# Scores and maxima in half-row form: two heads stacked in each half of the rows, maxima in neighbouring pairs

## The reference, cut to what matters

```python
q = (query @ Wq + bq).reshape(B, Nq, H, D).transpose(0, 2, 1, 3)   # H = 16 heads, D = 8
k = (key_value @ Wk + bk).reshape(B, Nkv, H, D).transpose(0, 2, 1, 3)
attn = jnp.einsum('bhqd,bhkd->bhqk', q, k) * scale
attn = jax.nn.softmax(jnp.clip(attn, -CLAMP, CLAMP), axis=-1)
x = jnp.einsum('bhqk,bhkd->bqhd', attn, v).reshape(B, Nq, Cq) @ Wo + bo
```

## Time and profile before

| what | value |
|---|---|
| time, median of 3 runs | 981.94 us (979.5 to 982.6) |
| profiled execution, its span | 981.2 us |
| span from the median | 0.7 us less |
| busy TensorE, VectorE, ScalarE, GpSimd | 934.3, 737.5, 647.0, 350.3 us |
| cross-attention | periods of some 22 us from about 70 us to about 770 us |

### The profile page before, as it was taken

The page is one execution under the profiler, slowest core; times in us unless marked ns, Lnnn a source line. Parts: engine busy times, 40 slices in busy tenths (PEclk is TensorE's granted clock), DMA queues, the critical chain, the costliest instruction groups (busy, mean ns, idle before and its releaser), DMA issues.

```text
span 981.2 us, 28874 instructions
## 1 busy us (share of the span) xinstructions
PE 934.3 (95%) x10535; PEld 753.6 (77%) x10535; DVE 737.5 (75%) x1426; ACT 647.0 (66%) x1081; POOL 350.3 (36%) x334
## 2 busy tenths in 40 slices
PE   6877999999999999999999999999999899999995
PEld 4645787877777777787777877778777678999894
DVE  6673777777777777777777777777788857777996
ACT  3654777777777777777777777777776444445554
POOL 6452352223233332222323333222231413112992
PEclk8897999999999999999999999999999899999998
DMA  6538566666555556666655555666654201002331
GB/s 140 116 75 197 119 143 135 145 136 138 131 118 118 118 125 138 140 136 137 136 128 118 118 118 128 140 138 137 138 121 96 66 1 44 23 22 83 130 113 41
DMA packets 43626, 111.45 MB, mean 114 GB/s; under 512 B 15491, under 2 KB 26053, under 8 KB 43461
## 3 DMA queue, kind: packets, MB, share of 16 engines
q1 hardware_dynamic: 43572, 110.77, 49.9%
HBM read 32.23 MB, written 1.89 MB: 35 GB/s over the span
## 4 chain that ended last, share of the span: by engine, by line
PE 90%; DVE 4%; ACT 2%; SPq 2%; issue 1%; DMA 1%; POOL 0%; ACTq 0%; DVEq 0%
PE psum L1590 18%; PE psum L1414 18%; PE psum L1655 13%; PE psum L1421 8%; PE psum L1426 8%; PE psum L1659 4%; PE psum L1682 3%; PE psum L1683 2%; PE psum L1684 2%; PE psum L1695 2%; PE psum L1694 2%; PE psum L1696 2%; PE psum L1545 1%; PE psum L1431 1%; SPq L395 1%
## 5 line engine op out<-in xcount | busy, mean ns | idle before, releaser
L946 DVE TENSOR_REDUCE arena<-psum 128x1 f32<-128x500 f32 x672 | 443.0, 671 | 176.9 <-PE psum L1414 176.7
L759 ACT ACTIVATE arena<-psum 125x896 f32<-125x896 f32 x384 | 348.1, 916 | 114.2 <-PE psum L1590 102.5
L1414 PE MATMUL psum<-K_hi,Q_bd 128*128 128x500 f32 x672 | 310.0, 470 | 7.0 <-DVE arena L946 4.2
L547 POOL TENSOR_TENSOR arena<-arena,K_hi 128x500 fp32r<-128x500 f32 x96 | 119.9, 1249 | 407.3 <-ACT K_hi L690 407.3
L1590 PE MATMUL psum<-Q_st,K_st 97*125 97x224 f32 x1536 | 243.7, 281 | 0.7 <-ACT arena L759 0.6
L1590 PEld LDWEIGHTS psum<-Q_st,K_st 97*125 97x125 f32 x1536 | 222.7, 190 | 23.1 <-issue 3.9
L1414 PEld LDWEIGHTS psum<-K_hi,Q_bd 128*128 128x128 f32 x672 | 128.2, 191 | 64.9 <-issue 27.1
L1655 PE MATMUL psum<-arena 125*25 125x168 f32 x3072 | 171.2, 313 | 0.2
L813 ACT ACTIVATE K_st<-psum 128x448 fp32r<-128x448 f32 x128 | 69.7, 544 | 79.2 <-PE psum L1684 77.7
L1659 PE MATMUL psum<-arena 125*9 125x56 f32 x3072 | 117.7, 214 | 0.0
L1659 PEld LDWEIGHTS psum<-arena 125*9 125x9 f32 x3072 | 94.5, 92 | 16.7
(11 more groups left out here) (250 smaller groups left out, 1052.4 us busy)
## 6 DMA issues: line engine op xcount, KB each, us to landing
K_st<-K_hi SPq DMA_DIRECT2D x256, 187.5 KB, 4.7
K_st<-arena SPq DMA_DIRECT2D x128, 187.5 KB, 3.4
arena<-in_ctx SPq DMA_DIRECT2D x32, 562.5 KB, 6.7
arena<-gate_rows SPq DMA_DIRECT2D x8, 896.0 KB, 4.4
arena<-in_L_ffn_W SPq DMA_DIRECT2D x16, 256.0 KB, 3.1
Q_st<-max_row SPq DMA_DIRECT2D x224, 0.5 KB, 1.7
arena<-OS_all SPq DMA_DIRECT2D x12, 168.0 KB, 4.1
x_rows<-x_all SPq DMA_DIRECT2D x1, 896.0 KB, 6.5
```

Of the source, the lines that this page charges most:

```text
L547: g.tensor_tensor(low.bitcast(F32R), low, K_hi[:, par, n * KB:n * KB + KB].bitcast(F32), ALU.subtract).then_inc(F["keys_low"], 1)
L759: a.activation(P2[c % NP].rearrange("p (n k) -> p n k", n=2), psum[0:CK, 2 + 2 * (c % 2):4 + 2 * (c % 2), 0:HQ // 2], ACT.Exp)\
L946: v.reduce_max(mx[:, n // NB, n % NB:n % NB + 1], bank_of(n)[:, 0:KB], AX.X).then_inc(F["piece_max_taken"], 1)
L1414: mm(bank_of(n)[:, 0:KB], Q_bd[:, par].rearrange("p h q -> p (h q)")[:, 128 * (n // NB):128 * (n // NB) + 128], K_hi[:, par, (n % NB) * KB ...
```

## The change

Half-row form for scores: the array's rows are used as two halves, 0 to 63 and 64 to 127. Each half of `K_st` holds, for each of four groups, two heads: 16 rows of high keys, the same again, 16 rows of low keys, and a row of ones (row 48 or 112), 49 rows. `Q_st` correspondingly; the mask is `two_heads`. A chunk is eight matmuls of 49 rows with 112 columns, the lower half to one bank, the upper to the other. `load_keys` issues 24 DMAs a batch, `load_row` 8, and the first fill of `Qs_all` 28 where it was 12, likewise that for the other batches. `load_row` now follows `stacked_spread`, as the stacking also writes rows 48 to 63.

Maxima: a block of rows whose heads lie all in the lower (blocks 0 to 2) or all in the upper half (4 to 6) is multiplied with that half of the rows alone; block 3 uses all rows. A new order sets a lower and an upper block of the same third next to each other, and the tables give both to the same chunk. Banks and waits of `piece` stay as they are, by index in the new order.

```diff
-EARLY_PIECES = {0: (9,), 1: (10,), 2: (11,), 3: (12,), 4: (14,), 6: (18,), 7: (20,), 9: (2,), 10: (4,), 11: (6,)}
-MID_PIECES = {3: (13,), 5: (15, 16), 6: (19,), 8: (0,), 9: (3,), 11: (7,)}
-LATE_PIECES = {5: (17,), 8: (1,), 10: (5,), 11: (8,)}
+EARLY_PIECES = {0: (9, 10), 1: (11, 12), 2: (13,), 3: (14, 15), 4: (16, 17), 6: (18, 19), 7: (20,), 9: (3, 4), 10: (5, 6), 11: (7, 8)}
+MID_PIECES = {8: (0,)}
+LATE_PIECES = {8: (1, 2)}
...
+PIECE_ORDER = ((3, 0), (0, 0), (4, 0), (1, 0), (5, 0), (2, 0), (6, 0),
+               (0, 1), (4, 1), (1, 1), (5, 1), (2, 1), (6, 1), (3, 1),
+               (0, 2), (4, 2), (1, 2), (5, 2), (2, 2), (6, 2), (3, 2))
+HALF, MAX_AT = 64, 3 * 2 * DH
+SPREAD = HALF + MAX_AT
+ROW_PARTS = RG + 1
...
-        Q_st = sb("Q_st", [DC + 1, 2, HG, 4, S], F32R)
+        Q_st = sb("Q_st", [128, 2, HG, 2, S], F32R)
...
                     for g in range(HG):
-                        sp.dma_start(K_st[32 * q:32 * q + 32, par, g, :].bitcast(F32), part[32 * g:32 * g + 32, :].bitcast(F32))\
-                          .then_inc(D_[f"{'klo' if q == 2 else 'khi'}{par}"], 16)
+                        for a in (0, HALF):
+                            sp.dma_start(K_st[a + 16 * q:a + 16 * q + 16, par, g, :].bitcast(F32), part[a + 16 * g:a + 16 * g + 16, :].bitcast(F32))\
+                              .then_inc(D_[f"{'klo' if q == 2 else 'khi'}{par}"], 16)
...
+                for a in range(2):
+                    row = Q_st[HALF * a + MAX_AT:HALF * a + MAX_AT + 1, par].rearrange("a g h q -> a (g h q)")
+                    for j in range(RG):
+                        lo, hi = max(128 * j, HQ // 2 * a), min(128 * j + 128, HQ // 2 * (a + 1))
+                        if lo < hi:
+                            sp.dma_start(row[:, lo - HQ // 2 * a:hi - HQ // 2 * a].bitcast(F32), max_row[j:j + 1, lo - 128 * j:hi - 128 * j].bitcast(F32)).then_inc(D_["mrow"], 16)
+            sp.wait_ge(F["ones_ready"], 2 + PRIME)
...
-            for q, o in enumerate((HIGH_AT, LOW_AT, HIGH_AT)):
+            for q, o in enumerate((HIGH_AT, LOW_AT, HIGH_AT, HIGH_AT)):
                 for g in range(HG):
-                    sp.dma_start(Qs_all[32 * q:32 * q + 32, g, 0:QC], query_half(0, o)[32 * g:32 * g + 32, :]).then_inc(D_["q"], 16)
+                    for a in ((0, HALF) if q < 3 else (0,)):
+                        sp.dma_start(Qs_all[a + 16 * q:a + 16 * q + 16, g, 0:QC], query_half(0, o)[a + 16 * g:a + 16 * g + 16, :]).then_inc(D_["q"], 16)
...
+                    sp.wait_ge(F["stacked_spread"], b + 2 + PRIME)
                     load_row(1 - par)
...
-                g.tensor_tensor(Q_st[0:DC, par], Qs_all[:, :, bass.ds(b * S, S)].unsqueeze(2).to_broadcast([DC, HG, 4, S]),
-                                four_heads[:].unsqueeze(1).unsqueeze(3).to_broadcast([DC, HG, 4, S]), ALU.mult).then_inc(F["stacked_spread"], 1)
+                g.tensor_tensor(Q_st[0:SPREAD, par], Qs_all[0:SPREAD, :, bass.ds(b * S, S)].unsqueeze(2).to_broadcast([SPREAD, HG, 2, S]),
+                                two_heads[0:SPREAD].unsqueeze(1).unsqueeze(3).to_broadcast([SPREAD, HG, 2, S]), ALU.mult).then_inc(F["stacked_spread"], 1)
...
-                v.reduce_max(mx[:, n // NB, n % NB:n % NB + 1], bank_of(n)[:, 0:KB], AX.X).then_inc(F["piece_max_taken"], 1)
+                j, third = PIECE_ORDER[n]
+                v.reduce_max(mx[:, j, third:third + 1], bank_of(n)[:, 0:KB], AX.X).then_inc(F["piece_max_taken"], 1)
...
-                mm(bank_of(n)[:, 0:KB], Q_bd[:, par].rearrange("p h q -> p (h q)")[:, 128 * (n // NB):128 * (n // NB) + 128],
-                   K_hi[:, par, (n % NB) * KB:(n % NB) * KB + KB], start=True, stop=True).then_inc(F["max_scores_made"], 1)
+                rows = slice(0, 128) if j == RG // 2 else slice(0, HALF) if j < RG // 2 else slice(HALF, 128)
+                mm(bank_of(n)[:, 0:KB], Q_bd[rows, par].rearrange("p h q -> p (h q)")[:, 128 * j:128 * j + 128],
+                   K_hi[rows, par, third * KB:third * KB + KB], start=True, stop=True).then_inc(F["max_scores_made"], 1)
...
                         for g in range(HG):
-                            last = mm(bank[2 + 2 * (c % 2) + g // 2][0:CK, 4 * S * (g % 2):4 * S * (g % 2) + 4 * S],
-                                      K_st[0:DC + 1, par, g, c * CK:c * CK + CK], Q_st[:, par, g].rearrange("p h q -> p (h q)"), start=True, stop=True)
+                            for a in range(2):
+                                rows = slice(HALF * a, HALF * a + MAX_AT + 1)
+                                last = mm(bank[2 + 2 * (c % 2) + a][0:CK, TT * g:TT * g + TT],
+                                          K_st[rows, par, g, c * CK:c * CK + CK], Q_st[rows, par, g].rearrange("p h q -> p (h q)"), start=True, stop=True)
```

More of the change, by code:

```diff
@@ L389, in _ @@
             sp.wait_ge(F["max_row_ready"], 1 + PRIME)
+            sp.wait_ge(F["stacked_spread"], 1 + PRIME)
             load_row(0)
@@ L392, in _ @@
             others = outputs_place[:, 0:(NQ - 1) * FIRST_WORDS].rearrange("p (n w) -> p n w", w=FIRST_WORDS)
-            for q, o in enumerate((HIGH_AT, LOW_AT, HIGH_AT)):
+            for q, o in enumerate((HIGH_AT, LOW_AT, HIGH_AT, HIGH_AT)):
                 for g in range(HG):
-                    sp.dma_start(Qs_all[32 * q:32 * q + 32, g, QC:B * S].rearrange("p (n c) -> p n c", c=QC), others[32 * g:32 * g + 32, :, o:o + QC]).then_inc(D_["qr"], 16)
+                    for a in ((0, HALF) if q < 3 else (0,)):
+                        sp.dma_start(Qs_all[a + 16 * q:a + 16 * q + 16, g, QC:B * S].rearrange("p (n c) -> p n c", c=QC),
+                                     others[a + 16 * g:a + 16 * g + 16, :, o:o + QC]).then_inc(D_["qr"], 16)
             sp.dma_start(x1_rows, x1_all[:]).then_inc(x1_saved, 16)
@@ L489, in _ @@
             keep(head_rows[:], [[DH, H]], DH - 1, -1)
-            for a3 in range(3):
-                step(g.tensor_copy(four_heads[32 * a3:32 * a3 + 32, :], head_rows[32 * a3:32 * a3 + 32, 4 * a3:4 * a3 + 4]))
+            step(g.tensor_tensor(head_sums[:], head_rows[:, 0:8], head_rows[:, 8:16], ALU.add))
+            step(g.tensor_tensor(head_sums[:, 0:4], head_sums[:, 0:4], head_sums[:, 4:8], ALU.add))
+            step(g.tensor_tensor(two_heads[:], head_sums[:, 0:2], head_sums[:, 2:4], ALU.add))
             keep(sum_rows[:].rearrange("p (g c) -> p g c", c=32), [[-32, 4], [0, 32]], -SUM, 1, ALU.not_equal, 1.0)
             pool.sem_inc(consts, 1)
-            step(g.memset(K_st[DC:DC + 1, 0, HG - 1].bitcast(F32), 1.0))
-            step(g.memset(K_st[DC:DC + 1, 1].rearrange("p g k -> p (g k)").bitcast(F32), 1.0))
+            step(g.memset(K_st[:, 0, HG - 1].bitcast(F32), 1.0))
+            step(g.memset(K_st[:, 1].rearrange("p g k -> p (g k)").bitcast(F32), 1.0))
+            pool.sem_inc(F["ones_ready"], 1)
             def later_constants():
@@ L765, in period @@
                         act.wait_ge(F["max_scores_made"], (b + 1) * PIECES + PRIME)
-                        act.wait_ge(D_[f"khi{par}"], (half + 1) * (16 * 2 * HG))
-                        act.wait_ge(D_[f"klo{1 - par}"], (half + (par + 1)) * (16 * HG))
+                        act.wait_ge(D_[f"khi{par}"], (half + 1) * (16 * 4 * HG))
+                        act.wait_ge(D_[f"klo{1 - par}"], (half + (par + 1)) * (16 * 2 * HG))
                         key_copy(b + 2, par, n, bank[7])
@@ L934, in normed @@
                 v.tensor_copy(x_hi[:, tokens(n)], bank[X_BANK[n]][:, 0:QC]).then_inc(P.S3["normed_copied"], 1)
-            v.memset(K_st[DC:DC + 1, 0, 0:HG - 1].rearrange("p g k -> p (g k)").bitcast(F32), 1.0).then_inc(F["ones_ready"], 1)
+            v.memset(K_st[:, 0, 0:HG - 1].rearrange("p g k -> p (g k)").bitcast(F32), 1.0).then_inc(F["ones_ready"], 1)
             dve.wait_ge(w_ps, 1)
@@ L1406, in piece @@
                     pe.wait_ge(F["queries_spread"], b + 1 + PRIME)
-                if n < NB:
-                    pe.wait_ge(F["keys_high"], b * NB + n + 1 + PRIME)
+                j, third = PIECE_ORDER[n]
+                if n % RG == 0:
+                    pe.wait_ge(F["keys_high"], b * NB + third + 1 + PRIME)
                 if n == 2:
@@ L1579, in period @@
                         if c == 0:
-                            pe.wait_ge(D_[f"khi{par}"], (half + 1) * (16 * 2 * HG))
-                            pe.wait_ge(D_[f"klo{par}"], (half + 1) * (16 * HG))
-                            pe.wait_ge(D_["mrow"], (b + 1) * (16 * RG))
+                            pe.wait_ge(D_[f"khi{par}"], (half + 1) * (16 * 4 * HG))
+                            pe.wait_ge(D_[f"klo{par}"], (half + 1) * (16 * 2 * HG))
+                            pe.wait_ge(D_["mrow"], (b + 1) * (16 * ROW_PARTS))
                             pe.wait_ge(F["stacked_spread"], b + 1 + PRIME)
                             if isinstance(b, int) and b == 0:
-                                pe.wait_ge(F["ones_ready"], 1 + PRIME)
+                                pe.wait_ge(F["ones_ready"], 2 + PRIME)
```

18 lines of the change are left out of this document (8 added, 10 removed).

## The result

The changed kernel takes 1177.36 us (median of 4 runs, 1167.43 to 1181.09); the kernel before takes 982.27 (4 runs, 979.5 to 983.05). The ratio is 1.199, 95% interval 1.1945 to 1.2036: slower, as forecast, but beyond the upper end of the range, 1160.

The account below looks back on a forecast made before the run. TensorE's list of work was taken to bound each period: -2.07 + 2.8 + 3.06 = +3.8, so 26.0. Then 981.2 + 16 + 110 + 2 gave 1109 us, own range 1085 to 1130, wider range 1020 to 1160.

Parts of the forecast that it names:

- Scores: no gain: TensorE's score matmuls: four half-row pairs still take four key loads 0.11 apart, 0.43 us a chunk as before.
- Rival two: Scores also halve, as half-row loads are quicker or overlap deeper: 1011 without change-over costs, 1077 with; chance 0.1.
- the 0.43: Cost in us of a chunk's scores on TensorE, taken unchanged, partly because loads into separate strips were said to overlap.
- Changes of division: 14 at 0.2 = 2.8: TensorE switching between half and whole rows: 14 new changes a period at 0.2 us, 2.8 a period.
- the walk's 26.0: Length in us of one batch's period, c0 to c0, from stepping through program order with the prices taken.
- Rival one: Changes between half and whole rows are free: periods of 23.8 us, total 1043; chance 0.2.
- Stalls: +3.06: Maximum pairs on two banks wait for VectorE in c1, c2, c3, c9, c11: 3.5 us a period, less 0.44 already there.
- the 2.07: Maxima on TensorE: nine half-row pairs save nine times 0.23 us, 2.07 a period, where both of a pair can start.
- Start: +16: SP's added DMA issues before the steady stretch: row goes at 70.2, ScalarE passes near 102; +15 to +17 us.
- SP and the new wait of `load_row`: SP's issues, about 21.5 us a period, stay hidden; the wait for `stacked_spread` was met long before.
- Rivals three and four: Three: halves run one after another, 1147 or near 1225, chance 0.12. Four: SP's 21.5 sets the period, 977, chance 0.05.

Follow-up runs that it names:

- e4: The changed kernel with VectorE reducing only the first 250 columns of each maximum piece, so waits are shorter: 1038.54 us.
- e5: The changed kernel with six added pairs of unread products (49 rows, 448 columns) in the long waits of chunks c2 and c9: 1106.73 us.
- e12: The changed kernel with the same six added pairs of unread products, but in chunks c3 and c4, where no long wait stands: 1314.07 us.
- e3: The kernel before with only the new tables, so whole-row maximum pieces go in pairs, no half rows: 1033.99 us.
- e11: The kernel before with the pair tables on whole rows, plus one more 512-column VectorE reduction ahead of the pieces of c1 and c9: 1050.36 us.
- e1: The changed kernel with old order and tables and every maximum piece on all rows, only scores in half rows: 1112.88 us.
- e7: The kernel before with one added 56-column product on 64 rows in the middle of each chunk's score matmuls: 1127.15 us.
- e8: The kernel before with one added 56-column product on 97 rows, like its neighbours, in each chunk's score matmuls: 1023.28 us.

## Why the prediction was right in its direction and wrong in its size

**The step that failed** is the one that was never written: durations of the steady stretch at granted clock 1.00 were carried over to a kernel whose steady stretch has another clock. That is worth the 79 us of the periods with falls. Without them the sum would be 981.2 + 20.4 + 86 + some 4 (an estimate of what the 8.9 of the last two periods would be without theirs) = 1092, inside the forecast's own range of 1085 to 1130. That falls are common only with the waits is shown by e4 and e5 (waits shortened or filled, order and operands of the rest kept) and e12 (the same products, elsewhere); that waits alone don't do it, by e3 and e11; that half-row scores alone don't, by e1. So it takes half rows and waits together to lose the clock period after period. Whether half-row scores or half-row pieces alone would do beside the waits stays open, and so does what the chip reacts to: all 29 periods of after have both waits and thirteen have no fall, and two falls of e5 come without a wait. The prediction had both ingredients, placed the waits where the clock falls, and asked only what each costs at full clock.

**Scores: no gain.** Right. The eight matmuls take 0.65 where four took 0.60. e1's 23 changes at the 0.148 of e7 less e8 make 3.4 of its 3.53 a period, which leaves 0.01 a chunk for the scores. e5 shows why: in c9 its last three pairs of 448 columns start at 415.90, 416.10 and 416.30, 0.20 apart as one such matmul streams, the two halves of a pair 0.01 apart, so halves do run together, while pairs of 112 columns stay 0.11 apart, as loads do. The Trainium skill (TensorEngine Tiling, Theoretical Speedup) promises up to twice the rate for a dimension of 64 or less: the pairs of 448 columns agree, those of 112 show nothing of it. Rival two is out. One argument for the 0.43 did not hold, though the figure did: that strip loads overlap. Eight loads of 25 columns and eight of 9 are 272 columns; at 0.11 for 128, if a load goes by its columns, they take 0.23 one after another and fit ahead of outputs 0.38 apart as well. It is the pairs here that show loads of two halves side by side.

**Changes of division: 14 at 0.2 = 2.8.** Right in kind, too dear: 0.148 (e7 less e8) and 0.153 (e1), so 2.1; this is nearly all that the walk's 26.0 is above the 25.2 at full clock. The Trainium skill (TensorEngine Tiling, Key Properties) has a change of mode drain the engine; these runs agree that it costs time, and whether it is a drain they do not show. Rival one, changes for nothing, is out.

**Stalls: +3.06.** At the predicted places (c1, c2, c3, c9, c11). What is left of 25.2 - 22.24 + 2.07 - 2.1 is 2.9; that is a remainder, not measured, and it takes the 2.07 as forecast; e4 gives a lower bound, 1.8. Of a period's nine pairs five start as one (c0 above, 0.45 for both); in c1, c3, c9 and c11 the second piece waits for its bank and starts 0.07 to 0.58 later (c1 above, 0.86 for both). After has 32.6 us in 82 such waits of TensorE's loads from 200 to 700 us, 4 to 5 a period, 14.6 in 23. The walk had VectorE too slow: from a pair's first maximum to the reciprocal behind it the trace has 1.18 and 1.11 (395.98 to 397.16, 397.92 to 399.03), where 1.35 was taken.

**Start: +16.** It was +20.4. SP and ScalarE at the start, against the earlier trace rows:

```profile
33.54 10.11 SPq L380 DMA_DIRECT2D K_st<-K_hi  x16
43.70 5.01 SPq L380 DMA_DIRECT2D K_st<-arena  x8
48.75 18.88 SPq L399 DMA_DIRECT2D arena<-arena  x28
...
70.05 4.96 SPq L389 DMA_DIRECT2D Q_st<-max_row  x8
75.05 18.91 SPq L410 DMA_DIRECT2D arena<-OS_all  x28
...
94.63 6.69 SPq L380 DMA_DIRECT2D K_st<-arena  x8
```

```profile
103.73 0.58 ACT L707 COPY arena<-psum 128x500 f32<-128x500 f32 x1 [15.13 <-DMA K_st<-arena]
```

The row goes at 70.05 (70.2 forecast), ScalarE passes at 103.73 (102). From there to the sums it takes 19.3 us, 15.8 before, at a mean granted clock of 0.75, 0.82 before: the part of the miss that is the clock's again.

**SP and the new wait of `load_row`** cost nothing in the steady stretch, as said: no wait for a DMA stands in TensorE's list of 275 to 340 us. Rivals three and four are out: halves do run together, and a period is far above 21.6.

## What to carry to other kernels

A period walked at one clock is a forecast only if the clock stays; where a change thins out what TensorE does (half rows) and in the same place makes it wait, price that stretch at the lower level too, and look at the PEclk line of the result before anything else. Splitting the array pays where streaming is the long part (pairs of 448 columns), not where 125 columns of weights are loaded for 112 that stream, and each change between half and whole rows takes 0.15 us, so half-row work wants to stand together. A pair that shares two banks with the pair before trades streaming time for waits on whoever empties them; no run here had more banks for the pieces.

## What the runs showed of the hardware that was not expected

- Steady work of one core ran at half the clock in a part of more than half of the periods (16 of 29), with TensorE 94% busy and never idle for more than 0.43 us at a time: after at 0.88 in the mean of 200 to 700 us, e12 at 0.79, while e11, which idles more and has waits up to 1.1, stays at 1.00.
- Added work can shorten a kernel: 12 products a period in the right place, 70.6 us less; the same products elsewhere, 136.7 us more.
- Loads and streams of two halves ran side by side (pairs 0.20 apart at 448 columns, the time of one such stream), yet a short product cost its load: 0.11 a pair at 112 columns, 0.096 for the one of 56.
